# First attention, steps 0 to 3: the order of the copies on ScalarE, of Q's projection on TensorE and of the output addition on VectorE

## The reference, cut to what matters

```python
Q = einsum('bse,hec->bhsc', X, Wq) + bq      # K alike: 128 columns a head, two halves of 64
V = einsum('bse,hed->bhsd', X, Wv) + bv      # 64 columns a head
A1 = einsum('bhqd,bhkd->bhqk', Q1, K1) * s   # A2 alike from the second halves
P = softmax(A1) - lam * softmax(A2)
O = einsum('bhqk,bhkd->bhqd', P, V)
Y = concat_of_heads(O) @ Wo + bo             # then a layer norm, gamma, beta, times 0.2
```

## Time and profile before

| | us |
|---|---|
| median of 3 runs | 1739.81 (1737.58 to 1742.07) |
| the profiled execution | 1746.17 |
| its span, first to last instruction | 1744.2 |
| TensorE busy in the span | 1572.3 (90%) |
| VectorE, ScalarE, GpSimd busy | 1339.7, 1283.2, 964.1 |
| mean granted TensorE clock | 0.956 of full speed |

### The profile page before, as it was taken

The page is one execution under the profiler, slowest core; times in us unless marked ns, Lnnn a source line. Parts: engine busy times, 40 slices in busy tenths (PEclk is TensorE's granted clock), DMA queues, the critical chain, the costliest instruction groups (busy, mean ns, idle before and its releaser), DMA issues.

```text
span 1744.2 us, 28177 instructions
## 1 busy us (share of the span) xinstructions
PE 1572.3 (90%) x10531; PEld 660.0 (38%) x10531; DVE 1339.7 (77%) x2075; ACT 1283.2 (74%) x2052; POOL 964.1 (55%) x661
## 2 busy tenths in 40 slices
PE   5899999999999999999999999996676899999986
PEld 2444443444444444444434444433452122222223
DVE  5686777777777777777777777777868999999946
ACT  4787888788888888788888788884343588888872
POOL 1798877777777777777777787782000000111112
PEclk8999999999999999999999999998687799999998
DMA  4110011101111011100110011100000000000001
GB/s 118 27 27 22 21 28 27 31 22 25 24 33 26 22 25 24 33 25 23 27 34 25 22 25 23 31 12 5 1 11 32 2 15 14 15 15 18 15 10 37
DMA packets 50434, 42.35 MB, mean 24 GB/s; under 512 B 26021, under 2 KB 39242, under 8 KB 50298
## 3 DMA queue, kind: packets, MB, share of 16 engines
q1 hardware_dynamic: 50298, 40.55, 9.6%
HBM read 20.27 MB, written 1.31 MB: 12 GB/s over the span
## 4 chain that ended last, share of the span: by engine, by line
PE 56%; DVE 20%; issue 12%; ACT 8%; POOL 1%; DMA 1%; SPq 1%; ACTq 0%; POOLq 0%; DVEq 0%
PE PS L1461 13%; PE PS L1437 12%; PE PS L1449 11%; DVE nmx L1025 9%; PE PS L1787 4%; PE PS L1485 4%; ACT ering L748 3%; PE PS L1754 2%; DVE mxp L1343 2%; PE PS L1504 2%; DVE yT L1067 2%; PE PS L1771 2%; PE PS L1727 1%; ACT ering L933 1%; ACT t L759 1%
## 5 line engine op out<-in xcount | busy, mean ns | idle before, releaser
L1025 DVE TENSOR_REDUCE nmx<-PS 128x1 f32<-128x1024 f32 x512 | 624.9, 1221 | 241.2 <-PE PS L1438 237.5
L567 POOL TENSOR_TENSOR ering<-ering 128x1024 f32<-128x1024 f32 x256 | 602.7, 2354 | 21.4
L748 ACT ACTIVATE ering<-PS,nmx 128x1024 f32<-128x1024 f32 x512 | 570.6, 1114 | 34.3 <-DVE nmx L1025 31.1
L565 POOL TENSOR_SCALAR ering<-ering,rho 128x1024 f32<-128x1024 f32 x256 | 286.3, 1119 | 247.3 <-DVE rho L1034 246.4
L1437 PE MATMUL PS<-region 64*128 64x512 f16 x1536 | 401.1, 381 | 18.2 <-ACT ering L748 14.2
L1438 PE MATMUL PS<-region 64*128 64x512 f16 x1536 | 401.2, 381 | 0.0
L1449 PE MATMUL PS<-ident,ering 128*128 128x128 f32 x2048 | 333.6, 286 | 41.9 <-ACT t L759 18.1
L1449 PEld LDWEIGHTS PS<-ident,ering 128*128 128x128 f32 x2048 | 218.2, 141 | 298.0 <-issue 198.1
L1343 DVE TENSOR_REDUCE mxp<-PS 128x2 f32<-128x1024 f32 x256 | 303.7, 1221 | 31.6 <-PE PS L1771 28.0
L933 ACT ACTIVATE ering<-PS 128x1024 f32<-128x1024 f32 x256 | 260.6, 1025 | 79.4 <-PE PS L1754 71.8
L1437 PEld LDWEIGHTS PS<-region 64*128 64x128 f16 x1536 | 115.0, 94 | 239.8 <-ACT ering L748 76.5
(11 more groups left out here) (286 smaller groups left out, 1856.5 us busy)
## 6 DMA issues: line engine op xcount, KB each, us to landing
region<-region SPq DMA_DIRECT2D x64, 256.0 KB, 3.6
osb<-scr SPq DMA_DIRECT2D x32, 128.0 KB, 3.0
rcp<-scr SPq DMA_DIRECT2D x32, 128.0 KB, 3.2
rcp<-scr SPq DMA_DIRECT2D x64, 64.0 KB, 2.0
x<-in_L_attn_X SPq DMA_DIRECT2D x4, 256.0 KB, 3.2
wq_raw<-in_L_attn_Wq SPq DMA_DIRECT2D x16, 64.0 KB, 3.1
wk_s<-in_L_attn_Wk SPq DMA_DIRECT2D x16, 64.0 KB, 1.9
wo_s<-in_L_attn_Wo SPq DMA_DIRECT2D x32, 32.0 KB, 2.5
```

The costliest lines, as they stand in the source:

```text
L565: P.tensor_scalar(e2, e2, rho[:, s:s + 1], 1.0, ALU.mult, ALU.mult).then_inc(s_scl_ok, 1)
L567: P.tensor_tensor(e1, e1, e2, ALU.subtract).then_inc(s_sub_ok, 1)
L748: A.activation((E1, E2)[p][s % 4], PS[:, bank:bank + 2, :].rearrange("p a b -> p (a b)"), ACT.Exp, bias=nmx[:, 2 * s + p:2 * s + p + 1], s ...
L1025: V.tensor_reduce(nmx[:, 2 * s + p:2 * s + p + 1], PS[:, bank:bank + 2, :].rearrange("p a b -> p (a b)"), AX.X, ALU.max, negate=True).then ...
```

## The change

Four orders change; no instruction is added or taken away.

- ScalarE, step 1: `high_k(n+1, 0)` moves from ahead of the first `keep_t` to behind it. Step 2's `high_k(n+1, 1)` stays ahead of it.
- ScalarE, step 2: the second `keep_t` moves ahead of `high_q`. (In the code the two lines change places.)
- VectorE, step 0: `add_out(n-2)` moves from ahead of the second maximum to behind it.
- TensorE, step 2: `project_q(n+1)` moves from ahead of the first `turn` to behind it.

```diff
@@ ScalarE
-                    if s in (1, 2) and nxt and own:
-                        high_k(n + 1, s - 1)
+                    if s == 2 and nxt and own:
+                        high_k(n + 1, 1)
...
                     if later:
                         keep_t(m, (s + 5) % 8, 0)
+                    if s == 1 and nxt and own:
+                        high_k(n + 1, 0)
                     if own:
                         exponent(n, s, 0)
                     if 3 <= s < 6 and n == 0:
                         keep_w(2 * s - 5)
+                    if later:
+                        keep_t(m, (s + 5) % 8, 1)
                     if s == 2 and nxt and own:
                         high_q(n + 1)
-                    if later:
-                        keep_t(m, (s + 5) % 8, 1)
                     if own:
                         exponent(n, s, 1)
@@ VectorE
                         weigh(n if s else n - 1, (n if s else n - 1) % 2, (s + 7) % 8)
-                    if s == 0 and n >= 2:
-                        add_out(n - 2)
...
                     if own:
                         maximum(n, s, 1)
+                    if s == 0 and n >= 2:
+                        add_out(n - 2)
@@ TensorE
-                    if s == 2 and nxt and own:
-                        project_q(n + 1)
...
                     if later:
                         turn(m, (s + 5) % 8, 0)
+                    if s == 2 and nxt and own:
+                        project_q(n + 1)
```

## The result

The kernel after takes 1719.76 us (median of 4 runs, 1712.33 to 1722.22), that before 1738.69 (4 runs, 1735.62 to 1742.07). The ratio is 0.9884, with an interval of 0.9847 to 0.992: 1.2% faster, 19 us, against a forecast of 1718.4 us and 21.4 us less. The profiled execution went from 1746.17 us to 1719.14, its span from 1744.2 to 1717.3. The sign, the size and the mechanism of the prediction held.

A forecast was written before the change was run, and what follows sets the result against it. TensorE was taken to bound each attention unit; 1.01 us won less 0.26 lost gives 0.75 a unit, 29 x 0.75 - 0.3 = 21.4 us, so 1739.8 becomes 1718.4 us; 8 in 10 range 1706 to 1729.

The forecast's parts named there:

- What bounds the unit: First attention: TensorE busy 34.19 of 35.85 us, full from step 4 into step 7; only idle in steps 1 to 3 winnable.
- Step 0, the addition, at 0: VectorE, step 0: the addition behind the second maximum has 0.4 us of cover before the scores of v = 3; gain 0.
- Step 1, a loss of 0.26: Step 1: K's later high copy delays its low part and the second K projection, losing 0.26 us per unit.
- Steps 2 to 4, a gain of 1.01: Steps 2 to 4: earlier copies and turns remove TensorE's waits, winning 1.01 us per unit.
- The new wait at v = 9: TensorE, second scores of step 4: they wait 0.18 us for the later exponent of step 3.
- The check list: Expected profile after: period 35.1 us, ScalarE's 1.42 us idle in step 2 gone, 0.7 to 0.9 before second K projection.
- The sum: Whole kernel: 29 units at 0.75 us won, less 0.3 for unit 3, giving 21.4 us.
- Unit 3: Unit of 39.72 us where constants' matmuls fill step 3's gaps; only step 1's loss remains, about 0.3 us.
- special units, 0, 3 and 31: Units without the full pattern: 0 turns nothing in these steps, 31 projects nothing, 3 has matmuls for constants.
- The one that ended slower: Rival: Q's later high copy delays step 3's exponent, every unit 0.56 us longer, 17 us, 1757; chance 0.04.
- Step 1 costs nothing: Rival: the high copy's lateness in step 1 is hidden or won back before v = 9; 29 us, 1711; chance 0.13.

The follow-up runs named there:

- experiment 5: Kernel after with the output addition put back ahead of the second maximum of step 0; period 35.01 us, one time of 1720.06 us.
- experiments 7 and 8: Kernel before, Q's projection behind first turn, K's first low part ahead of step 1's weights; 7 also moves the addition: 1698.37 us; 8 does not: 1702.14 us.
- experiment 6: Kernel before with only K's first high copy moved behind the first copy of step 1; period 36.12 us, one time of 1750.74 us.
- experiment 3: Kernel after with K's first high copy put back ahead of the first copy in step 1; 1711.96 us, ratio 0.9832 to before.
- experiment 4: Kernel after with Q's high copy put back ahead of the second copy in step 2; 1713.2 us, ratio 0.9832.
- experiment 1: Kernel before with only Q's projection moved behind the first turn of step 2; 1704.86 us against 1742.67, ratio 0.9795.
- experiment 2: Kernel before with only ScalarE's step 2 swap, second copy ahead of Q's high copy; period 35.05 us, one time of 1716.67 us.

## Why the prediction was right, step by step

- **What bounds the unit.** Right: the stretch from step 4 stays full (16.80 of 16.80 us), and every kernel's period moved by what TensorE's waits in steps 1 to 4 and the one unseen distance moved.
- **Step 0, the addition, at 0.** Right in this kernel, shown by experiment 5 (35.01 with and without). It had 0.4 of cover by the forecast and ends at 530.70, 0.48 ahead of the scores of v = 3 (531.18). It is not 0 everywhere: once the low part no longer holds K's projection, it is worth 34.43 - 34.32 = 0.11 (experiments 7 and 8).
- **Step 1, a loss of 0.26.** Right: 0.27 alone (experiment 6) and 0.27 in company (experiment 3). The chain turn, copy, high copy, low part, projection took 3.54 us in the kernel after (529.84 to 533.38), as worked out, against 3.28 before. The wait ahead of the projection was forecast as 0.7 to 0.9 and is 0.80.
- **Steps 2 to 4, a gain of 1.01.** The mechanism was right, the size 0.1 too small. From the first scores of step 2 to the second of step 4 it is 9.85 us (534.39 to 544.24), forecast 9.95, before 10.96. The mis-sized term is the distance from a turn to Q's projection, taken as the 0.59 of a turn followed by scores; it measured 0.49 (535.15 to 535.64). It was the order that no row of before showed.
- **The new wait at v = 9.** Forecast 0.18, measured 0.18; it belongs to Q's high copy going behind the second copy, since it went when that swap was undone (experiment 4, 0.19).
- **A wording that failed.** The check list said that ScalarE's 1.42 in step 2 would be gone. The first copy's wait went, but 1.13 us of the same idle time now stands ahead of the second copy.
- **The sum.** The period was to fall by 0.75 and fell by 0.84. From unit 1's copy to unit 30's, the two traces differ by 22.4 us (81.34 to 1124.93 before, 78.45 to 1099.64 after), forecast 21.4. Two terms inside it miss in opposite directions. 27 regular distances fell by 0.84 each, 22.6 in all against 20.3 by the forecast, and the one that holds unit 3's constants grew by 0.22, forecast 0.3. But the first, from unit 1's copy to unit 2's, did not shrink (35.85 in both), which the prediction had counted as 0.75.
- **Unit 3.** The forecast of a loss of 0.3 fits, as long as kernels with the same clock there are compared: with a granted clock of 0.96 it took 39.72 before and 40.02 in experiment 6, 39.65 in experiment 3 and 39.94 after. In experiments 1, 2, 4 and 5 the clock there was 1.00, and the same distance took 38.14 to 38.36. So where the clock falls is worth some 1.5 us in the time of one execution, and the period says more about a move than the time does. Why it fell in some kernels and not in others is not shown.
- **Unit 1, the part of the sum that failed.** The swap on ScalarE is what takes its gain: with Q's high copy put back (experiment 4) the distance is 34.82, like all others, and it is 34.66 in experiment 1, but 36.08 in experiment 2, the swap alone. It is not the only move that costs there: experiments 7 and 8, without it, took 34.83 and 35.26 against their periods of 34.32 and 34.43. VectorE and GpSimd carry extra work there, and VectorE's differs in length. Of the three rows the first two are of the kernel after, the third of the kernel before (the two instructions are L1002 there):

```profile
90.61 3.05 DVE L1004 TENSOR_SCALAR yc<-fb,fcol 128x256 f32<-128x256 f32 x2
90.55 1.84 POOL L593 IOTA t<- 128x2048 f32 x1
```

```profile
94.82 1.70 DVE L1002 TENSOR_SCALAR yc<-fb,fcol 128x256 f32<-128x256 f32 x2
```

Behind Q's high copy GpSimd's iota starts at 12.10 in the kernel after and at 12.07 before; VectorE gets to its two instructions at 12.16 instead of 13.48, and yet ends them at 15.21 and 15.18. The exponent that waits for the maximum behind them stands still for 1.51 us instead of 0.17, and TensorE takes 0.83 more from there into the next unit's step 0 than one unit on (92.94 to 101.80, 8.86 us, against 8.03). So the prediction's list of special units, 0, 3 and 31, lacked unit 1. That the iota is what holds VectorE is an inference from these times; no kernel was made without it.
- **Rivals.** The one that ended slower needed v = 9 to have less than 0.56 of cover. In experiment 2, where only ScalarE's swap makes that exponent late, the unit still wins 0.81, so the cover was there. "Step 1 costs nothing" fell by experiments 3 and 6. What the prediction did not list as a case is the one that matters most for the reader: the projection's move alone, at 1.29 a unit, is better than the four together.

Outside the sum, the profiled executions differ by 27.0 us, 4.6 more than the distances above explain: 2.9 of it lies ahead of unit 1's copy and 1.6 behind unit 30's, where the late steps of unit 30 itself stand. In the first and the second 40 us of the kernel after the granted clock was 0.91 and 1.00, in those of the kernel before 0.87 and 0.91. So TensorE spent more of the kernel's start at its upper level, 2.4 GHz, in the execution after. Whether the change has a part in that is open: no kernel was made for it, and the medians (19 us apart, with an interval of 14 to 27) do not need it.

## What to carry to other kernels

Walk the chain of each move with the starts of the trace and keep the waits of all engines in the same table: all eight kernels here landed within 0.04 us of the period so worked out for them, once the one unseen distance had been measured. Two moves that remove the same wait do not add, and the second can cost: after the projection had moved, ScalarE had just the gap that Q's high copy needed, and putting the copy of the turn first made it wait through that gap. So try each move of a bundle alone. And a copy that another engine turns into the release of a bank (here high copy, low part, projection) was worth 0.27 us a unit ahead of a copy that is not ready yet (experiments 3 and 6).

## What the runs showed of the hardware that was not expected

From a turn's start to that of the float32 projection behind it are 0.49 us, to that of float16 scores 0.58 (535.15 to 535.64, and 538.21 to 538.79); the projection behind a turn is drawn 1.88 us long, behind scores 1.98 (511.39 in the earlier trace rows).

VectorE's two comparisons in unit 1 ended 1.26 to 1.28 us behind the end of GpSimd's iota in all ten kernels, though they began from 12.16 to 13.72 us behind Q's high copy and took 1.70 to 3.05 us. The first of the two is alone 0.58 us long before and 1.92 after.

And a wait can stand in a TensorE timeline with no bracket: the 0.18 ahead of the second scores of step 4 shows only as a distance of 0.83 between starts that were 0.65 apart, since the last matmul ahead of them, started at 543.85, is drawn to 544.23.
